# Expert steps of a routed feed-forward layer: 128-column weight blocks as the stationary operand of gate and up, rows moving

## What is computed

```python
x = x + _L0_xattn_ref(_layernorm(x, axis=-1), ctx_2048, ...)
x = x + _L0_ffn_ref(_layernorm(x, axis=-1), ...)

def _L0_ffn_ref(hidden_states, gate_w, w_gate_proj, w_up_proj, w_down_proj):   # E, I, H = 32, 192, 512
    x = hidden_states.reshape(-1, H)
    router_logits = x @ gate_w.T
    masked_w, _count = _masked_routing(router_logits)      # softmax over the 8 highest, else 0
    g = jnp.einsum('th,eih->tei', x, w_gate_proj)
    u = jnp.einsum('th,eih->tei', x, w_up_proj)
    h = jax.nn.silu(g) * u
    h = h * masked_w[:, :, None]
    out = jnp.einsum('tei,ehi->th', h, w_down_proj)
```

## Time and profile before

| | us |
|---|---|
| median of three timed runs | 1113.05 |
| lowest and highest of them | 1113.04, 1119.22 |
| span of the profiled execution | 1115.7 |
| TensorE busy in it | 1007.8 (90%) |
| ScalarE | 775.1 (69%) |
| GpSimd | 736.9 (66%) |
| VectorE | 713.2 (64%) |
| time in indirect DMA adds on GpSimd, L741 | 250.4, 148 of them |

### The profile page before, as it was taken

One profiled execution on the slowest core, in us unless ns is written; L12 is line 12 of the kernel. 1 busy time (PEld: TensorE's weight loads), 2 busy tenths in 40 slices (PEclk: granted clock), 3 DMA queues, 4 the chain that ended last, 5 costly groups with the idle time before them and its releaser, 6 DMA issues.

```text
span 1115.7 us, 29688 instructions
## 1 busy us (share of the span) xinstructions
PE 1007.8 (90%) x7192; PEld 481.3 (43%) x7193; DVE 713.2 (64%) x1354; ACT 775.1 (69%) x1800; POOL 736.9 (66%) x663
## 2 busy tenths in 40 slices
PE   6589999999999999973199999999999999999996
PEld 2122222222222222221066666666666666666663
DVE  7878899999999888756434445544545553553521
ACT  2178888888888887662166676777677767777674
POOL 3034477777777774456557777778777777778775
PEclk9599999999999999886599999999999999999998
DMA  7313444444444333310187888898798898889674
GB/s 237 120 56 107 125 127 126 127 126 128 126 127 127 117 112 120 111 39 20 43 285 177 230 225 214 206 230 229 173 238 224 203 221 223 210 198 235 123 141 87
DMA packets 88882, 175.58 MB, mean 157 GB/s; under 512 B 23658, under 2 KB 40426, under 8 KB 84594
## 3 DMA queue, kind: packets, MB, share of 16 engines
q0 software_dynamic: 38080, 75.58, 31.5%
q1 hardware_dynamic: 50736, 99.26, 28.0%
q10 hardware_dynamic: 4, 0.02, 0.0%
HBM read 118.30 MB, written 61.58 MB: 161 GB/s over the span
## 4 chain that ended last, share of the span: by engine, by line
PE 42%; issue 3%; DVEq 2%; DVE 2%; DMA 1%; ACTq 1%; POOL 1%; ACT 0%; POOLq 0%; SPq 0%
PE ps L1697 23%; PE ps L1705 5%; PE ps L1723 2%; PE ps L1726 2%; PE ps L1724 2%; PE ps L1727 2%; PE ps L1725 2%; DVEq L349 1%; PE ps L1713 1%; DVE w_lo L1352 1%; PE ps L1715 1%; PE ps L1714 1%; ACTq L349 1%; DVE w_hi L1347 1%; POOL expert_rows L600 0%
## 5 line engine op out<-in xcount | busy, mean ns | idle before, releaser
L1036 DVE TENSOR_REDUCE mx<-ps 128x2 f32<-128x1024 f32 x256 | 303.7, 1222 | 37.3 <-PE ps L1669 34.4
L1697 PE MATMUL ps<-w_hi,o_raw 128*128 x1200 | 318.2, 327 | 0.0
L767 ACT ACTIVATE pr<-ps 128x512 f32<-128x512 f32 x512 | 278.4, 602 | 49.8 <-PE ps L1646 48.6
L741 POOL DMA_INDIRECT out<-v,s_idx x148 | 250.4, 1692 | 86.5 <-issue 40.3
L723 POOL DMA_INDIRECT pr<-normalised_tokens,g_idx x155 | 168.8, 1089 | 61.6 <-issue 18.2
L1697 PE MATMUL ps<-w_lo,o_raw 128*128 x600 | 196.2, 327 | 0.0
L757 ACT ACTIVATE o_raw<-ps 128x1024 f16<-128x1024 f16 (+1 forms) x183 | 174.9, 956 | 3.0 <-PE ps L1658 1.6
L1364 DVE SCALAR_TENSOR_TENSOR rope_b<-rope_a,stacks,ps 128x192 f32<-128x192 f32 x150 | 61.6, 411 | 147.9 <-ACT rope_a L923 108.0
L1697 PEld LDWEIGHTS ps<-w_hi,o_raw 128*128 128x128 f16 x1200 | 117.7, 98 | 85.8 <-issue 1.0
L600 POOL DMA_INDIRECT expert_rows<-rows,rowi x128 | 127.1, 993 | 37.2 <-issue 36.8
L1658 PE MATMUL ps<-pr,v 128*32 128x512 f32 x1024 | 140.3, 621 | 1.6 <-ACT pr L767 1.2
(11 more groups left out here) (161 smaller groups left out, 1464.0 us busy)
## 6 DMA issues: line engine op xcount, KB each, us to landing
stage<-in_expert_w SPq DMA_DIRECT2D x32, 1280.0 KB
stacks<-qk_parts SPq DMA_DIRECT2D x128, 96.0 KB, 2.7
w_lo<-in_x SPq DMA_DIRECT2D x32, 256.0 KB, 2.9
w_lo<-in_ctx SPq DMA_DIRECT2D x32, 256.0 KB, 5.8
qk_parts<-qk SPq DMA_DIRECT2D x32, 256.0 KB
qk_parts<-qk SPq DMA_DIRECT2D x32, 128.0 KB
out<-x SPq DMA_DIRECT2D x16, 256.0 KB, 4.9
normalised_tokens<-x2s SPq DMA_DIRECT2D x16, 256.0 KB, 2.5
```

Of the source, the lines that this page charges most:

```text
L741: nc.gpsimd.indirect_dma_start(out_rows, bass.IndirectOffsetOnAxis(s_idx[:, s.slot(4), 0:1], 0), y_sb[:, s.slot(4), :], None, bounds_check ...
L767: nc.scalar.activation(pr[:, n % 8, :], bank(f"s{n}"), ACT.Exp, scale=DH ** -0.5).then_inc(exp_done, 1)
L1036: V.tensor_reduce(mx[:, b.slot(2), at:at + 3:2, tile], bank(f"m{n}"), AXX, ALU.max).then_inc(mx_done, 1)
L1697: last = mm(ps[:, s.slot(2), 0:2 * INTER], xt[:, s.slot(2), at:at + P], w[:, cols], start=(m == 0), stop=(m == 3 * KT - 1))
```

## The change

Gate and up swap their operands. A block of 128 weight columns is now the stationary operand and the transposed rows move, 128 of them. The 384 columns are laid out on the host in another order, [gate 0 to 127, up 0 to 127, gate 128 to 191 and up 128 to 191], and make three blocks; with 4 blocks of the inner dimension and 3 combinations there are 36 matmuls a step. The result has the weight columns on the partitions, so the gated rows come out transposed and feed the down product as they are: `transpose_h` and `read_ht` are gone, and the down product moves from step s - 2 to step s - 1. The last 64 columns of gate and up lie side by side on the partitions, so the silu, the product, and both halves of h are two instructions each. A row's routing weight can't be applied to the gated rows by partition any more; `read_y` applies it as the scale of its copy. GpSimd's add waits on two looked-up counters and one fixed one, not on four looked-up ones.

```diff
-        sil = rope_a[:, :, 0:INTER]
-        hf = rope_b[:, :, 0:INTER]
-        hs = rope_s[:, :, :].bitcast(F16)[:, :, 0:2 * INTER]
+        sil = rope_a[:, :, 0:2 * P]
+        hf = rope_b[:, :, 0:2 * P]
...
-                before = fields(gp, s, 0, 4, 16 * (STEPS // 4 + 1), table=before_tab, width=4)
+                one, two = (s + -1).slot(4), (s + -2).slot(4)
+                first = min(one, two)
+                before = fields(gp, s, first, 2, 16 * (STEPS // 4 + 1), abs(one - two), table=before_tab, width=4)
...
-                for q in range(4):
-                    gp.wait_ge(added[q], before[q])
+                need(gp, added[(s + -3).slot(4)], (s + -3).rounds(4, 16, 32))
+                for q, adds in zip(sorted((one, two)), at_least_none):
+                    gp.wait_ge(added[q], adds)
...
             def silu(s):
-                nc.scalar.activation(sil[:, s.slot(2), :], ps[:, s.slot(2), 0:INTER], ACT.Silu, scale=1.0 / WSCALE).then_inc(sil_done, 1)
+                nc.scalar.activation(sil[:, s.slot(2), 0:P], ps[:, s.slot(2), 0:P], ACT.Silu, scale=1.0 / WSCALE)
+                nc.scalar.activation(sil[SIDE:P, s.slot(2), P:2 * P], ps[0:SIDE, s.slot(2), 2 * P:3 * P], ACT.Silu, scale=1.0 / WSCALE).then_inc(sil_done, 1)
...
             def high_of_h(s):
-                need(act, ht_mm, s.count(1, -1))
-                copy(hs[:, s.slot(2), 0:INTER], hf[:, s.slot(2), :]).then_inc(hhi_done, 1)
-
-            def read_ht(s):
-                act.wait_ge(ht_mm, s.count(1, 1))
-                need(act, d_mm, s.count(1, 0) if not isinstance(s.k, int) or s.count(1) > 1 else 0)
-                copy(ht[:, s.slot(2), :, :], ps[:, 4 + s.slot(2), :].bitcast(F16)[:, 0:3 * P].rearrange("p (b t) -> p b t", b=3)).then_inc(ht_out, 1)
+                need(act, d_mm, s.count(1, -2))
+                copy(ht[:, s.slot(4), 0, :], hf[:, s.slot(2), 0:P])
+                copy(ht[SIDE:P, s.slot(4), 2, :], hf[SIDE:P, s.slot(2), P:2 * P]).then_inc(hhi_done, 1)
...
-                copy(y_sb[:, s.slot(4), :], ps[:, 6 + s.slot(2), :], 1.0 / (WSCALE * PSCALE)).then_inc(y_out, 1)
+                copy(y_sb[:, s.slot(4), :], ps[:, 6 + s.slot(2), :], place_of[:, bass.ds(at + 2, 1)].bitcast(F32)).then_inc(y_out, 1)
...
-                V.scalar_tensor_tensor(hf[:, s.slot(2), :], sil[:, s.slot(2), :], place_of[:, bass.ds(at + 2, 1)].bitcast(F32),
-                                       ps[:, s.slot(2), INTER:2 * INTER], ALU.mult, ALU.mult).then_inc(h_done, 1)
+                V.scalar_tensor_tensor(hf[:, s.slot(2), 0:P], sil[:, s.slot(2), 0:P], PSCALE / WSCALE, ps[:, s.slot(2), P:2 * P], ALU.mult, ALU.mult)
+                V.scalar_tensor_tensor(hf[SIDE:P, s.slot(2), P:2 * P], sil[SIDE:P, s.slot(2), P:2 * P], PSCALE / WSCALE,
+                                       ps[SIDE:P, s.slot(2), 2 * P:3 * P], ALU.mult, ALU.mult).then_inc(h_done, 1)
...
-                m = 0
-                for k in range(KT):
-                    cols = bass.ds(slot + k * 2 * INTER, 2 * INTER)
-                    for px, w in ((HI, w_hi), (HI, w_lo), (LO, w_hi)):
-                        at = (px * KT + k) * P
-                        last = mm(ps[:, s.slot(2), 0:2 * INTER], xt[:, s.slot(2), at:at + P], w[:, cols], start=(m == 0), stop=(m == 3 * KT - 1))
-                        m += 1
+                for block in range(3):
+                    m = 0
+                    for k in range(KT):
+                        cols = bass.ds(slot + (k * 3 + block) * P, P)
+                        for px, w in ((HI, w_hi), (LO, w_hi), (HI, w_lo)):
+                            at = (px * KT + k) * P
+                            last = mm(ps[:, s.slot(2), block * P:(block + 1) * P], w[:, cols], xt[:, s.slot(2), at:at + P], start=(m == 0), stop=(m == 3 * KT - 1))
+                            m += 1
...
             def down(s, slot):
-                pe.wait_ge(ht_out, s.count(1, 1))
+                pe.wait_ge(hlo_done, s.count(1, 1))
...
             def step(s):
-                first, last = s + 2, s + -2
+                first, last = s + 2, s + -1
...
-                if (s + -1).live():
-                    transpose_h(s + -1)
...
-    gu = np.concatenate([gp, up], axis=1).transpose(0, 2, 1).reshape(E, KT, P, 2 * INTER).transpose(0, 2, 1, 3).reshape(E, P, -1)
+    gu = np.concatenate([gp[:, 0:P], up[:, 0:P], gp[:, P:], up[:, P:]], axis=1).transpose(0, 2, 1).reshape(E, KT, P, 2 * INTER).transpose(0, 2, 1, 3).reshape(E, P, -1)
```

More of the change, by code:

```diff
@@ L339, in step_loop, with fields @@
             tail(Turn(last, GROUP, GROUP, STEPS))
-        def fields(eng, s, f, n, hi, apart_by=1, lo=0, table=tab, width=STEP_FIELDS):
+        def fields(eng, s, f, n, hi, apart_by=1, lo=0, table=tab, width=STEP_FIELDS, waited=False):
             at = s.count(width, f)
@@ L348, in fields @@
                 view = table[0:1, bass.DynSlice(at, n, apart_by)]
+            if waited:
+                return nc.values_load_multi_w_load_instructions(view, engines=[eng.engine], min_val=lo, max_val=hi)[1]
             return nc.values_load_multi_w_load_instructions(view, engines=[eng.engine], min_val=lo, max_val=hi,
@@ L551, in load_weights @@
                 with sp.If(load > 0):
[L552 removed]
+                    nxt, = fields(sp, s, NEXT, 1, E - 2, waited=True)
                     at, = fields(sp, s, STAGE, 1, WCOLS)
@@ L726, in _ @@
                 gather(Turn(0, d, GROUP, STEPS))
+            at_least_none = [gp.alloc_register(f"adds_before{n}") for n in range(2)]
             def add(s):
@@ L971, in step @@
             def step(s):
-                ahead, at, behind = s + (GROUP + LEAD + 1), s.off % 4, s + -2
+                ahead, at, behind = s + (GROUP + LEAD + 1), s.off % 4, s + -1
                 if (s + 1).live():
                     silu(s + 1)
-                if (s + -1).live():
-                    read_ht(s + -1)
                 if (s + 3).live():
@@ L988, in step @@
                     rows_to_add(behind, past[at])
-                    read_y(behind)
+                    read_y(behind, past[at])
                 rows_to_gather(ahead, places[at])
             def tail(end):
-                ends = fields(act, end + -2, ROW, 2, LAST_PLACE, STEP_FIELDS)
-                read_ht(end + -1)
-                for n in range(2):
-                    rows_to_add(end + (n - 2), ends[n])
-                    read_y(end + (n - 2))
+                at, = fields(act, end + -1, ROW, 1, LAST_PLACE, STEP_FIELDS)
+                rows_to_add(end + -1, at)
+                read_y(end + -1, at)
                 silu(end + 1)
@@ L1379, in step @@
                 if ahead.live() and (first == 0 or not splits):
-                    for n, flag in enumerate(fields(dve, ahead, SPLIT, 4 - first, (E - 1) * FREED + STEPS + 1, STEP_FIELDS)):
+                    for n, flag in enumerate(fields(dve, ahead, SPLIT, 4 - first, (E - 1) * FREED + STEPS + 1, STEP_FIELDS, waited=True)):
                         splits[first + n] = flag
-                if (s + 2).live() and (first == 0 or not places):
-                    for n, place_at in enumerate(fields(dve, s + 2, ROW, 4 - first, LAST_PLACE, STEP_FIELDS)):
-                        places[first + n] = place_at
-                next_weights(splits[first], lambda: hidden(s + 2, places[first]) if (s + 2).live() else None)
+                next_weights(splits[first], lambda: hidden(s + 2) if (s + 2).live() else None)
             step_loop(dve, step, lambda end: None)
@@ L1706, in transpose_x @@
                 last.then_inc(xgt_mm, 1)
-            def transpose_h(s):
-                pe.wait_ge(hlo_done, s.count(2, 2))
-                need(pe, ht_out, s.count(1, -1))
-                o = ps[:, 4 + s.slot(2), :].bitcast(F16)
-                h = hs[:, s.slot(2), :]
-                nc.tensor.transpose(o[:, 0:P], h[:, 0:P], ident)
-                nc.tensor.transpose(o[:, P:2 * P], h[:, 2 * P:3 * P], ident)
-                nc.tensor.transpose(o[:, 2 * P:3 * P], h[:, P:2 * P], ident).then_inc(ht_mm, 1)
             def down(s, slot):
-                pe.wait_ge(ht_out, s.count(1, 1))
+                pe.wait_ge(hlo_done, s.count(1, 1))
                 need(pe, y_out, s.count(1, -1))
                 y = ps[:, 6 + s.slot(2), :]
-                h = ht[:, s.slot(2), :, :]
+                h = ht[:, s.slot(4), :, :]
                 d0, d1 = slot + DOWN, slot + (DOWN + T)
@@ L1748, in tail @@
             def tail(end):
-                slot, = fields(pe, end + -2, SLOT, 1, slots)
-                transpose_h(end + -1)
-                down(end + -2, slot)
                 slot, = fields(pe, end + -1, SLOT, 1, slots)
```

29 lines of the change are left out of this document (14 added, 15 removed).

## The result

| | before | changed |
|---|---|---|
| median of the timed runs, us | 1116.13 (1113.04 to 1119.69) | 1277.95 (1275.56 to 1281.5) |
| ratio to before | | 1.1446, 95% interval 1.1407 to 1.1484 |
| span of the profiled execution, us | 1115.7 | 1279.7 |

The change costs 14.5%. The forecast was 1275 us, its range 1245 to 1360.

What follows compares the result with a forecast made beforehand. The array bounds before, TensorE's own queue after: 2.9 - 0.2 + 1.92 + 0.15 = 4.77 us a step against 3.668, +163 us over 148 steps, less 1.2 at the end, forecast 1275 us; range 1245 to 1360.

Steps and rivals of the forecast that it cites:

- The bound before, and the queue's 3.05 us: Expert steps before: the array bounds at 3.67 us; TensorE's queue has about 3.05 us of work, hidden by 0.6.
- +1.92 us for eight more groups: Gate and up in TensorE's queue: 12 groups of address calculations a step, not 4, at 0.24 us each extra group.
- The sum, 4.77 us a step: TensorE's queue after the change: 4.77 us of work a step, 1.2 over the array's 3.54, sets the step.
- The end, -1.2 us: Behind the last gate and up: one down product (1.08) and the transposes (0.17) less, so 1.2 us saved.
- The loop turn, 0.15 us: TensorE's queue at the loop's turn, once in four steps: 0.6 us, so 0.15 us a step.
- The array catches up before the twelfth group: Gate and up: the array, some 0.7 us behind, catches up with the queue, at 0.167 against 0.24 us a group.
- ScalarE, VectorE, GpSimd at nothing: Work changes on the other three engines lie beside a step of 4.77 us and cost or gain nothing.
- Rival 1: Expert steps: the queue's work stays hidden and the array stays the bound, step 3.57 us, 1097 us in all; 7%.
- Rival 2: Expert steps: TensorE's clock falls to 1.2 GHz because of pauses; 1360 us if in a quarter of steps; 15%.
- Rival 3: Gate and up: 98 ns weight loads don't hide behind 128-column matmuls, array's step 5.05 us, 1317 us in all; 4%.

Runs made afterwards that it cites:

- after_one_load: Changed kernel with TensorE's queue reading the step table once in four steps, seven slots at once, not two slots every step; ratio to before 1.1389.
- fixed_all: Changed kernel with all stationary blocks of gate and up from a constant tile, taking 24 address calculations from each step; ratio to before 1.0298.
- branch_down_last_one_load: Changed kernel with gate and up written out four times at fixed addresses behind branches, down product last, one table load in four steps; ratio to before 1.0706.

## Why the prediction was right

- **The bound before, and the queue's 3.05 us.** Held. The 12 increments of 0.15 us added to the kernel before raised its step by 1.30 us, so some 0.5 us were hidden, where the prediction had 0.6.
- **+1.92 us for eight more groups.** Held. The four calculations taken away were worth 0.111 us each in the step, two a group; with three matmuls passed on a group comes to 0.23 to 0.27 us in the timeline, against 0.24. A group of 0.24 with two calculations of 0.111 leaves almost nothing for the matmuls.
- **The sum, 4.77 us a step.** Measured 4.744. 148 x (4.744 - 3.668) = 159, and 1115.7 + 159 is 1275 against a span of 1279.7. The five us left are in several places. The first product of gate and up starts 1.2 us later than before (558.05 against 556.84), the first eleven steps lose another 1.3, the products of gate and up are 150 (two steps more than the 148, so 149 distances), and the end is the next point. That the forecast came within 3 us is in part luck: the step was taken 0.026 us too long, some 4 us over 148, and start and end too short. In the first steps the clock once stood at half (from 584 to 588 us):

```profile
584.00:588.00 4.00, 4.00 (x31) 2.95 (x29) 0.58 (x2) 2.51 (x6) 2.52 (x2) 0.57 0.95 328
588.00:592.00 4.00, 4.00 (x60) 3.32 (x57) 1.16 (x4) 2.95 (x8) 1.36 (x3) 1.00 0.83 171
```

- **The end, -1.2 us.** Mis-sized, on the wrong side: from the last product of gate and up to the end of the span it is 13.16 us before and 13.46 after, 0.3 more. Behind the last product of gate and up the queue has 2.5 us of branches (L333 and L335, 1266.30 to 1268.81) and a table load to do ahead of the last down product. Before, it was ahead of the array there: the same branches began at 1099.88, with matmuls up to 1102.84. After, the array waits for them:

```profile
1269.61 0.39 PE L1712 MATMUL ps<-w_hi,x 128*128 x1 [3.10 <-issue]
```

- **The loop turn, 0.15 us.** Pauses of 1.31 at a turn against 0.58 and 0.68 beside it: about 0.7, 0.17 a step.
- **The array catches up before the twelfth group.** It did at the tenth.
- **ScalarE, VectorE, GpSimd at nothing.** Held for the changed kernel. GpSimd and ScalarE wait for TensorE more than before (in the stretch of 600 us, 136.5 us ahead of the gathers and 162.1 ahead of the silu and the copies to xt; before, 0.6 us ahead of the gathers and 42.1 ahead of the silu and the copies to ht, in 460 us), VectorE waits for ScalarE. It would not have held for a faster one: without calculations the waits for VectorE and ScalarE set the time, and GpSimd's part, with the bounded table values, cost 0.1 to 1%.
- **Rival 1** (the array stays the bound) did not come about, and its price of 1097 us was wrong too: without any calculation in gate and up the kernel took 1.030 of before. The step at fault in the price is the reading that the queue "runs ahead, at a pace of its own". It does, for 15 matmuls. I had seen the lead in us and taken it for a property of the queue, where it belongs to the length of the matmuls.
- **Rival 2** (the clock) did not come about at pauses of 0.6 and 1.3 us, apart from the one fall at 584; it did at 21 of 34 turns of after_one_load.
- **Rival 3** (the load does not hide) fell: the second and third group of a block start 0.17 us apart, and where the queue has no calculations 36 matmuls run without a break (fixed_all):

```profile
821.27 2.17 PE L1695 MATMUL ps<-o_raw,ch 128*128 128x128 f16 x36
```

  Less the last one's own 0.22 that is 1.95 / 35 = 0.056 us each. The 81 ns that the Trainium skill states for a stream of pairs of load and matmul at 128 columns ("TensorE: Matmul & The Clock Gate", section "Back-to-back issue gap") did not show here in blocks of 36.

## What to carry to other kernels

Before cutting matmuls shorter, count what TensorE's own queue does between them: here a run-time address cost 0.11 us, and it was free only as long as all that the queue had to do in a step took less time than the matmuls of the step. The queue's lead is a number of matmuls, so the same table load or loop turn that vanished behind 15 of 384 columns shows behind 15 of 128. And a bound taken away shows the next one, so the gain of removing it should be read from what the other engines have left, not from the array's work alone.

## What was not expected of the hardware

- At the table load the array never had more than 15 matmuls left to start, whether they were of 128, 384 or 512 columns (132 and 131 steps of two kernels). In fixed_all it had 17 at the first instruction of the queue behind each block of 36. The Trainium skill ("TensorE: Matmul & The Clock Gate", section "Architectural detail: the array is 16× 32×32, not 1× 128×128") gives TensorE's queue a depth of 64; counted as pairs of load and matmul, 17 are 34 instructions, and no step counted here shows more.
- A table load costs by the value: 0.30, 0.53 and 1.73 us for one, two and seven. Some take longer: in fixed_all 50 of 141 between 590 and 1145 us took 0.6 to 2.1 us for two. GpSimd was in a gather (L724) during 45 of these 50 and during 27 of the other 91; whether the gather is the cause is not shown. In the changed kernel none of 127 was long.
- A semaphore increment between two transposes set them 0.15 us apart, against 0.055 without.
- The clock fell to half at 21 of the 34 turns of after_one_load, with pauses of 2.5 us and more. In branch_down_last_one_load, with pauses of 1.1 to 2.3 us at its turns, it fell at 6 of 33 (pauses of 1.8 to 2.3); behind the pause that ends at 916.5:

```profile
917.50:920.50 3.00, 3.00 (x31) 3.00 (x29) 0.60 (x3) 1.40 (x4) 2.32 (x3) 0.50 0.88 260
```

  Pauses of 0.6 to 1.3 us in every step for 600 us left it at 1.00 in the changed kernel.
